# Two chained attention layers on one core: score rows, row biases and small exponentials placed later in the engines' lists

## The reference

```python
h1 = _ln(x, ln1_g, ln1_b)
x = _attn(h1, h1, a1_wq, ..., d_q1, d_k1, d_v1, d_w1) + x
h2 = _ln(x, ln2_g, ln2_b)
x = _attn(h2, context, a2_wq, ..., d_q2, d_k2, d_v2, d_w2) + x
h3 = _ln(x, ln3_g, ln3_b)
a, g = jnp.split(h3 @ ff_w1 + ff_b1, 2, axis=-1)
x = a * jax.nn.gelu(g, approximate=False) @ ff_w2 + ff_b2 + x
...
scores = jnp.einsum('bhqd,bhkd->bhqk', rope(q), rope(k)) / math.sqrt(HD) + attention_mask
hidden = x + (softmax(scores) @ v) @ Wo
x = _rmsnorm(hidden, ln2_w)
return hidden + (silu(x @ Wgate) * (x @ Wup)) @ Wdown
```

## Time and profile before

| | |
|---|---|
| median of 3 runs | 2611.18 us (2611.0 to 2615.15) |
| the profiled execution | 2606.43 us, span 2604.6 us |
| PE busy | 2006.9 us (77%) |
| DVE busy | 1807.6 us (69%) |
| ACT busy | 1137.0 us (44%) |
| POOL busy | 944.2 us (36%) |
| one step in the middle | 142.6 to 147.5 us, PE busy 115 to 121 us of it |
| mean granted TensorE clock | 0.87 of full |

### The profile page before, as it was taken

One profiled execution on the slowest core, in us unless ns is written; L12 is line 12 of the kernel. 1 busy time (PEld: TensorE's weight loads), 2 busy tenths in 40 slices (PEclk: granted clock), 3 DMA queues, 4 the chain that ended last, 5 costly groups with the idle time before them and its releaser, 6 DMA issues.

```text
span 2604.6 us, 41636 instructions
## 1 busy us (share of the span) xinstructions
PE 2006.9 (77%) x10552; PEld 1439.3 (55%) x10552; DVE 1807.6 (69%) x3327; ACT 1137.0 (44%) x1906; POOL 944.2 (36%) x1628
## 2 busy tenths in 40 slices
PE   3556477978788787888788787878787787878786
PEld 2323255655556565656556565656555565656665
DVE  1456768677777868677877868677777868685532
ACT  1234453545344553545454554545353545444211
POOL 1213334344443434343443434343433424343212
PEclk8666688999989898998989898998889898989888
DMA  7577453453636353443536363543545353634010
GB/s 234 114 133 145 90 120 73 82 123 75 129 73 133 63 123 74 97 106 74 130 73 132 65 135 61 104 99 74 121 73 124 66 130 60 129 60 105 9 40 4
DMA packets 749785, 251.18 MB, mean 96 GB/s; under 512 B 661244, under 2 KB 742896, under 8 KB 749360
## 3 DMA queue, kind: packets, MB, share of 16 engines
q1 hardware_dynamic: 746287, 249.54, 45.6%
q10 hardware_dynamic: 3328, 0.01, 0.1%
HBM read 88.62 MB, written 22.40 MB: 43 GB/s over the span
## 4 chain that ended last, share of the span: by engine, by line
PE 39%; DVE 18%; issue 16%; SPq 12%; ACT 6%; DMA 5%; POOL 3%; DVEq 1%; ACTq 0%; POOLq 0%
PE work L1389 17%; PE work L1399 14%; SPq L541 4%; DMA PT<-Pn 3%; ACT E L894 3%; DVE scaled_row L1050 3%; PE rowps L1460 3%; DVE Pn L1057 2%; PE outps L1445 2%; DVE hids L1197 1%; POOL scs L794 1%; SPq L532 1%; DVE st L1073 1%; DMA xa<-in_x 1%; DVE xs L1187 1%
## 5 line engine op out<-in xcount | busy, mean ns | idle before, releaser
L1050 DVE TENSOR_SCALAR_CACHE_REDUCE scaled_row<-rowps,der 128x1024 uint8<-128x1024 f32 x512 | 654.6, 1279 | 322.8 <-PE rowps L1460 322.6
L894 ACT ACTIVATE E<-rowps,ebias,der 128x1024 f32<-128x1024 f32 x512 | 615.2, 1203 | 405.0 <-DVE scaled_row L1050 311.4
L1057 DVE TENSOR_SCALAR Pn<-E,rowinv 128x1024 int16<-128x1024 f32 x512 | 390.9, 764 | 164.1 <-DMA PT<-Pn 140.1
L728 POOL TENSOR_TENSOR rowden<-rowsum,raw 128x1 f32<-128x1 f32 x512 | 118.7, 232 | 957.5 <-ACT E L894 956.2
L1460 PE MATMUL rowps<-KC,QP 16*128 16x512 bf16 x1024 | 219.7, 426 | 242.1 <-ACT E L894 232.1
L731 POOL TENSOR_TENSOR rowinv<-rowden,minus 128x1 f32<-128x1 f32 x512 | 332.0, 648 | 91.6 <-POOL rowden L728 91.6
L1460 PEld LDWEIGHTS rowps<-KC,QP 16*128 16x128 bf16 x1024 | 49.0, 92 | 410.6 <-ACT E L894 281.6
L1389 PE MATMUL work<-hTs,ff_w_sb 128*128 128x256 f32 x1024 | 263.8, 413 | 13.0 <-ACT hTs L870 13.0
L1389 PEld LDWEIGHTS work<-hTs,ff_w_sb 128*128 128x128 f32 x1024 | 204.6, 206 | 60.4 <-issue 16.0
L1554 PE MATMUL work<-K,hids 128*128 128x154 f32 x1024 | 156.3, 305 | 28.8 <-DVE scs L1211 18.8
L1554 PEld LDWEIGHTS work<-K,hids 128*128 128x128 f32 x1024 | 141.4, 194 | 46.2 <-DVE scs L1211 25.1
(11 more groups left out here) (142 smaller groups left out, 3281.2 us busy)
## 6 DMA issues: line engine op xcount, KB each, us to landing
VW<-vw_dram SPq DMA_DIRECT2D x32, 640.0 KB, 4.8
K<-k_dram SPq DMA_DIRECT2D x16, 616.0 KB, 4.2
KC<-k_dram SPq DMA_DIRECT2D x128, 64.0 KB, 2.4
VB<-v_dram SPq DMA_DIRECT2D x64, 128.0 KB, 3.2
PT<-Pn SPq DMA_TRANSPOSE x512, 3.1
V<-v_dram SPq DMA_DIRECT2D x16, 320.0 KB, 3.9
vw_dram<-scs SPq DMA_DIRECT2D x32, 154.0 KB
K<-k_dram SPq DMA_DIRECT2D x16, 308.0 KB, 3.1
```

Source lines behind the costliest of these rows:

```text
L728: nc.gpsimd.tensor_tensor(rowden[:, n:n + 1], rowsum[:, n:n + 1], raw[:, DW1:DW1 + 1], ALU.mult).then_inc(row_den.sem, 1)
L894: nc.scalar.activation(E[:, slot, :], rowps[n % 2][:], ACT.Exp, bias=ebias[:, n:n + 1], scale=der[:, AL1:AL1 + 1], accum_out=rowsum[:, n:n ...
L1050: nc.vector.tensor_scalar(scaled_row[:, n % 2, :], rowps[n % 2][:], der[:, NAL1:NAL1 + 1], 3.0e38, ALU.mult, ALU.min, accum_out=ebias[:, n ...
L1057: nc.vector.tensor_scalar(Pn[:, n % 2, :], E[:, ring(n)[0], :], rowinv[:, n:n + 1], 255.0, ALU.mult, ALU.min).then_inc(row_round.sem, 1)
```

## The change

Five places change, and no instruction is added or removed.

- PE: row n+2 stands between the halves 2n and 2n+1 instead of ahead of 2n (`attn_pe`).
- DVE: the bias of n+1 opens tile n, and the rounding n-1 stands between the halves (`attn_dve`). Counted for one row tile, both come one half tile later among the chains' work.
- ACT: the small exponentials of both cross attentions are due 1.2 and 1.0 half tiles later (L930, L970).
- DVE: the second layer's sums are due 1.0 and 0.8 half tiles later (L1224).
- POOL: the first two divisions are due 0.4 later (L803).

```diff
@@ high_pool
-                        yield at("sc1", 3) + 0.6 + t
+                        yield at("sc1", 3) + 1.0 + t
                         probs(t)
@@ low_act
-                yield at("sc2", 2 * n + 1) + 1
+                yield at("sc2", 2 * n + 1) + 2.2
@@ high_act
-                yield at(f"sc{n // 2}", 2 * (n % 2) + 1) + 1.2
+                yield at(f"sc{n // 2}", 2 * (n % 2) + 1) + 2.2
@@ attn_dve
-                for n in range(AHEAD):
-                    biggest(n)
+                biggest(0)
             for n in range(ROWT):
+                if tiles(parts, n + 1):
+                    biggest(n + 1)
+                beside.until(2 * n)
                 if tiles(parts, n - 1):
                     rounded_probs(n - 1)
-                beside.until(2 * n)
-                if tiles(parts, n + AHEAD):
-                    biggest(n + AHEAD)
                 beside.until(2 * n + 1)
@@ high_dve, sums
-                    yield at(f"sc{hf}", 3) + (0.3 if hf == 0 else 1.8) + t
+                    yield at(f"sc{hf}", 3) + (1.3 if hf == 0 else 2.6) + t
```

## The result

The changed kernel takes 2672.8 us (median of four runs, 2671.5 to 2676.0) against 2611.1 us before: 1.0238 times as long, with a 95% interval of 1.022 to 1.0255. The sign was forecast, the size was not: 2630 was predicted, with 2658 as the upper end of the range. In what follows, medians and ratios leave out an execution that took over 1.5% longer than the fastest of its kernel, which concerns one of e2's four (2687 us).

What follows compares the result with a forecast made beforehand. No engine is full; a step is a chain across engines, with SP the bound from `down` to `wo`. Terms of +1.55 us over 14 steps gave +22 us on 2606.4, some 2632 as measured; 2630 was predicted, range 2578 to 2658.

Steps and rivals of the forecast that it cites:

- (f): At `tr1`: bias 24 ahead of the second output projection's taking out, bias 25 ahead of the norm; +0.9 us a step.
- rival 3: Slower by the clock too: fewer but longer PE waits put all steps in the longer form, +1.6 us more; 2655, chance 0.10.
- The first stretch: From `down` to `wo`: SP is the bound, issuing some 40 us of transposes and loads from `down`'s store to `oT`.
- (a): At `down`: bias 29, rounding 27 and bias 30 stand ahead of its taking out on DVE, delaying the store; +0.9 us.
- (b): At `wo`: bias 9 waits for the row behind `wo` and delays the taking out, through to `pt0`; +1.6 us.
- (c) to (e): `pt0` to `gate`: rows no longer block or split PE work, -1.6; `pt1`'s copy later, +0.4; at `gate`, -0.65 us.
- (e): At `gate`: large exponential 18 ahead of `tr3`'s taking out, -1.2; small exponential +0.55 later; together -0.65 us.
- (g): Second layer's later small exponentials and sums: `q2` up to 2 us sooner, worth nothing while POOL is later; 0.
- The rival *faster: The waits were the bound: `pt0` follows `q2`, not POOL, and `wo` finds `oT` landed; -2.3 us a step, 2579, chance 0.30.
- The signs: Expected in the profile after: PE's exponential waits under half, larger waits at `pt0` and `wo`, store some 3.5 us behind `down`'s matmuls.

Runs made afterwards that it cites:

- e2: Kernel before with DVE's list alone changed (bias n+1 opens the tile, rounding n-1 between the halves), PE's rows early as before; 2651.7 us, ratio 1.0144.
- e11: Changed kernel with POOL's last product of `up` and `gate` (L826) moved behind L761 instead of ahead of L1086; 2654.7 us, ratio 1.0184.
- e14: Changed kernel with idle identity transposes on PE, 14 in the wait ahead of `tr1` and 5 ahead of `g`; 2636.5 us, ratio 1.0088.
- e17: Changed kernel with row 29, bias 29 and rounding 27 early, and the taking out of `down` behind them, ahead of bias 30; 2680.7 us, ratio 1.0281.
- e3: Kernel before with PE's rows and DVE's list both changed, all constants as before; 2679.3 us, ratio 1.0287.
- e4: Kernel before with the constants alone changed (small exponentials, sums and divisions later); 2597.6 us, ratio 0.9968.
- e16: Kernel before with the later constants and idle identity transposes on PE in five waits (`pt0`, `tr3`, `gate`, `tr1`, `g`); 2596.5 us, ratio 0.9951.
- e12: Kernel before with the later constants, and on DVE the taking out of `down` ahead of bias 30 and rounding 28; ratio 0.9958.
- e15: Changed kernel with L1109 (taking out of the second output projection) ahead of bias 24 and L1086 ahead of bias 25 on DVE; 2646.2 us, ratio 1.0135.

## Why the prediction was wrong

The chain and the sign were right, the sum was not. Two steps of the prediction failed most: (f), the way to `tr1`, was put at +0.9 us and measured 2.06, since L1086 was taken at its old length (e11); and the clock, kept out of the sum as rival 3, costs 1.3 us a step ahead of `down` (e14). At the ends of the steps, PE's later rows were costed at nothing. Here are its steps in order, against the eight middle steps.

**What bounds the kernel.** Right in kind: no engine is full, the step is a chain, and the waits that went bought nothing. The first stretch was given to SP alone, from the store on. It is a near tie of two ways, SP's list and PE's way by the feed-forward, and the change lengthened both, by 1.1 and 2.3 us; e17 shows it, since it brought the store 3.3 us forward and `wo` only 0.5.

**(a)** +0.9 forecast. `down` to store went from 10.34 to 11.44 us, as worked out, and `down` to `wo` grew by 1.2 us in the middle steps, which fits. It is not the only holder of that time, as e17 shows: the other is in the sentence that costed PE's later rows "at nothing, and at +1 if the cover is thinner". The exponential that needs rounding 30 was named there, and its 1.6 to 2.3 us were not. In the last four steps `down` to `wo` grew by 3.9 us; PE does not wait for `oT` there at all (0.1 to 0.8 us before, 0 after), so this loss is that of the rows. The mechanism was in the prediction, its cover was not looked at: the four last steps have no `pre` work and SP is done early in them.

**(b)** +1.6, with (a) +2.5 up to `pt0`. Measured 1.79 from `wo` to `pt0`, 3.0 with the stretch ahead. At `wo`, as forecast: bias 9 starts 4.33 us behind the start of `wo`, and the taking out behind it.

```profile
1148.49 3.75 PE L1398 MATMUL work<-a_wo_sb,oT 128*128 128x256 f32 x8 [3.25 <-DMA oT<-OS]
1152.82 1.28 DVE L1050 TENSOR_SCALAR_CACHE_REDUCE scaled_row<-rowps,der 128x1024 uint8<-128x1024 f32 x1 [4.38 <-PE rowps L1459]
1154.03 0.69 DVE L1109 TENSOR_TENSOR xs<-work,xs 128x512 f32<-128x512 f32 x1
```

The taking out itself comes 1.9 us later behind the start of `wo` (mean of the eight steps). The stretch hides one thing more. In each of the eight steps a rounding 3.7 us ahead of `pt0` lasts 1.68 us, beside POOL's first division; the rounding at this place lasted 0.83 before. DVE's sum and POOL's second division, for which `pt0` waits, stand behind it:

```profile
1170.54 1.22 POOL L803 TENSOR_TENSOR pps<-scs,rsum 128x616 f32<-128x616 f32 x1
1170.62 1.68 DVE L1057 TENSOR_SCALAR Pn<-E,rowinv 128x1024 int16<-128x1024 f32 x1
```

In e3, without the later constants, this long rounding is gone and the stretch is 25.05 us instead of 25.58. No run takes it away alone.

**(c) to (e)** -1.85 together. `pt0` to `gate` gave 1.06 back. Part of (e) went on: `gate` started sooner, but `pt2` behind it waits for POOL's last cast, 1.0 to 1.4 us, where it waited 0.6 us for ACT, so that `gate` to `wo2` is 0.6 us longer. Against e3, the later constants gave 1.5 us up to `gate` and lost 1.4 behind it (32.36 and 18.34 us there, 30.84 and 19.70 in the changed kernel).

**(f)** +0.9 was the step of the sum that failed most: 2.06 from `wo2` to `g`. The order was read rightly (bias 24 ahead of the taking out, bias 25 ahead of L1086), the length of L1086 was taken as it was. After:

```profile
1227.51 1.28 DVE L1050 TENSOR_SCALAR_CACHE_REDUCE scaled_row<-rowps,der 128x1024 uint8<-128x1024 f32 x1 [0.82 <-PE rowps L1459]
1228.72 0.69 DVE L1109 TENSOR_TENSOR xs<-work,xs 128x512 f32<-128x512 f32 x1
1232.44 1.28 DVE L1050 TENSOR_SCALAR_CACHE_REDUCE scaled_row<-rowps,der 128x1024 uint8<-128x1024 f32 x1
1233.64 1.71 DVE L1086 TENSOR_SCALAR xns<-xs,mv,rs 128x256 f32<-128x256 f32 x2
1233.94 1.26 POOL L826 TENSOR_TENSOR hids<-hids 128x512 f32<-128x512 f32 x1
1235.41 0.66 PE L1381 MATMUL work<-ident,xns 128*128 128x128 f32 x4 [2.99 <-DVE xns L1086]
1237.18 3.78 PE L1388 MATMUL work<-hTs,ff_w_sb 128*128 128x256 f32 x8 [1.11 <-ACT hTs L870]
```

The move put L1086 beside a product of POOL, and it lasts 1.71 us for 0.72. e11 took that away alone: this stretch fell from 12.15 to 10.96 us, and the kernel by 18 us.

**(g)** 0 forecast. The constants as a whole are worth 8 to 10 us (e4), about what (e) alone was thought to give, but not at the place named: in the table e4's stretch to `gate` is not shorter than before (32.33 against 31.89 us). What is shorter there is `g` to `down`, 7.94 against 9.12 us, at the higher clock level in every step. And in the changed kernel the later division is one side of the collision shown under (b).

**The clock.** Rival 3 was right in kind and had 0.10: a wait that grows from 1.07 to 3.0 us stands ahead of `tr1` in every step, and `g` behind it starts at the lower level each time. That is 1.3 us a step from `g` to `down` in the middle steps, and e14 shows that up to 2.4 are to be had there. Its price of 1.6 was near that, but the step got longer in another way: six of the eight steps started `g` at the lower level before too, at 9.5 us from `g` to `down`; after, all eight do, and stay there longer (10.0 to 10.9 us). The Trainium skill (TensorE: Matmul & The Clock Gate, HAM oscillation) was cited for this rule; its own case is a long wait for a DMA in each round of a loop. The changed kernel bears it out at this place; the kernel before and e4, with the same waits and either level, show that a wait of this length alone does not settle it. Over a step, PE's busy time went from 119.3 to 121.4 us for the same instructions, so at most some 2.1 of the 5.9 us are the clock, if all of it lies on the chain. In e16, however, filled waits raised the mean granted clock to 0.90 and gained nothing beyond e4, so how the levels are dealt out over a step stays open.

**Sum.** +1.55 a step was forecast and 5.9 measured in the middle steps, 3.5 in the last four. Of the 4.3 missing in the middle: 1.3 are the clock ahead of `down`, 1.2 step (f), 0.8 less given back in (c) to (e), 0.6 behind `gate`, 0.2 in (b) and 0.3 ahead of `wo`. The rival *faster* rested on `pt0` following `q2`; `q2` came 1.7 us sooner behind the start of `wo` and `pt0` 1.8 us later, so it fell as its own test said.

**The signs.** Two of them did not come as written. PE's waits for exponentials fell from 232 to 131 us and not to less than half. The store comes 4.4 us behind the end of `down`'s matmuls, where 3.5 was forecast against 3.2 before; the terms of (a), 0.9 us later and matmuls that end 0.3 sooner, give 4.4 by themselves, so the sign was mis-added and (a) was not.

Three versions beat both kernels, all with the constants and without the new lists: e4 (0.9968) and, no further within their intervals, e12 (0.9958) and e16 (0.9951).

## What to carry to other kernels

Cost a moved instruction not only by what stands behind it, but by what the others run beside it at its new place, and by the buffer that it frees: here a rounding half a tile later held up an exponential, a row and a feed-forward three engines on. Before a stretch is given to one queue, look for the second-longest way to the same wait; a place that is shortened on one of two nearly equal ways gives little (e17: 0.5 of 3.3 us). And look at coupled lists as one: rows, biases and roundings half a tile later cost 9.1%, 3.9% and 3.3% alone and 2.9% together. Not every addition helps, though: biases and roundings together, without the rows, cost 1.4%, less than all three.

## What the runs showed of the hardware

**DVE and POOL hold each other up, one instruction at a time.** Over the 512 roundings of the kernel after, 480 last 0.75 us in the mean, and the 32 that start while a POOL operation on two tensors of 128x512 or 128x616 runs last 1.27, up to 1.78; the bias, which reads PSUM, lasts 1.28 us in both cases. POOL pays too: its cast L779 lasts 1.03 us in the kernel after and 0.70 before. The Trainium skill (SBUF — State Buffer, SBUF: two separate sides) has this as a port pair that DVE and POOL lock for a whole instruction; the rows fit. The two instructions of L1086 last 0.7 us together alone, and 1.1 (e15), 1.2 (once a step before) or 1.7 us (after), by how much of POOL's operation is left when they come; with the product behind them (e11) they are back at 0.7.

**A wait can be paid twice.** PE's 3.0 us ahead of `tr1` and 1.1 ahead of `g` are followed by 8 matmuls in 3.78 us that take 1.99 when the wait is filled with transposes of the identity (e14). With 1.07 and 0.79 us of wait at the same two places the 8 matmuls took 1.99 us in every step of e4, and in the kernel before 3.5 to 3.6 in six middle steps and 1.99 in two. The same trick at `pt0`, `tr3` and `gate` gained nothing in sum (e16); no run here tells why.
